# Graph convolution over 32 batches on one core: units in pairs of two batches, class rows read from 32 lanes, a ring of seven PSUM banks

## What is computed

```python
h = relu(layernorm(x, axis=-1))                 # x: 32 x 256 x 1024
# per batch: fv = h.mean(axis=1); sim = outer(fv, fv) / |fv|^2
# A = top 9 of each row of sim, without the first; symmetric; diagonal 1
y = relu((A / deg) @ (h.T @ W.T + b1))          # W = adj, 256 x 256
z = (A / deg) @ (y @ W.T + b2)
out = x + z.T
```

## Time and profile before

| | |
|---|---|
| median of 3 runs | 511.9 us (511.42 to 513.54) |
| the profiled execution | 514.48 us, of which the span is 512.7 |
| granted TensorE clock | 0.976 on the mean, 1.00 from 108 us on |
| PE busy | 449.6 us (88%) |
| VectorE busy | 428.0 us (83%) |
| ScalarE busy | 267.1 us (52%) |
| GpSimd busy | 206.4 us (40%) |
| chain that ended last | VectorE 44%, PE 23%, issue 11%, ScalarE 10%, GpSimd 8% |

### The profile page before, as it was taken

How to read it: one execution, slowest core, us unless ns; L and a number is a source line. 1 busy time by engine, 2 the same in 40 slices (tenths; PEclk the granted TensorE clock), 3 DMA queues, 4 the chain that set the end, 5 groups by cost and what they waited for, 6 DMA issues and landing times.

```text
span 512.7 us, 7375 instructions
## 1 busy us (share of the span) xinstructions
PE 449.6 (88%) x2188; PEld 200.9 (39%) x2188; DVE 428.0 (83%) x784; ACT 267.1 (52%) x561; POOL 206.4 (40%) x873
## 2 busy tenths in 40 slices
PE   0655599896998899999999899999999899999996
PEld 0112244333443344444444344444444444444442
DVE  5999879998899997999799988999799857853354
ACT  2975575347772377456863387356754453014300
POOL 1526463603537135623736335603744341414100
PEclk9986789999999999999999999999999999999999
DMA  8980000258003770087104760188006400250025
GB/s 296 383 352 1 1 1 2 82 193 291 10 1 130 256 271 1 1 319 269 71 0 166 257 236 1 58 272 320 11 0 225 168 19 1 82 216 31 1 115 214
DMA packets 19400, 68.20 MB, mean 133 GB/s; under 512 B 1824, under 2 KB 2464, under 8 KB 19360
## 3 DMA queue, kind: packets, MB, share of 16 engines
q1 hardware_dynamic: 19360, 67.73, 36.2%
HBM read 34.17 MB, written 33.55 MB: 132 GB/s over the span
## 4 chain that ended last, share of the span: by engine, by line
DVE 44%; PE 23%; issue 11%; ACT 10%; POOL 8%; POOLq 3%; DMA 1%; SPq 0%; DVEq 0%; ACTq 0%
PE ps L375 18%; DVE bn L905 10%; DVE hl L927 7%; DVE xs L946 7%; DVE hl L933 6%; POOL gat L709 4%; ACT hf L521 4%; ACT hl L530 3%; PE ps L387 3%; POOLq L706 2%; DVE idx L969 2%; DVE fv L961 2%; ACT hl L542 2%; DVE kind L978 1%; DVE fv L973 1%
## 5 line engine op out<-in xcount | busy, mean ns | idle before, releaser
L375 PE MATMUL ps<-hl,wh 128*128 128x512 f16 x1024 | 308.0, 383 | 29.6 <-DVE wl L1100 11.3
L375 PE MATMUL ps<-hl,wl 128*128 128x512 f16 x512 | 195.6, 382 | 0.0
L375 PEld LDWEIGHTS ps<-hl,wh 128*128 128x128 f16 x1024 | 97.7, 99 | 155.0 <-DVE xs L946 17.7
L521 ACT ACTIVATE hf<-xs,nbias,rstd 128x1024 f32<-128x1024 f32 x64 | 79.0, 1234 | 74.2 <-POOL nbias L695 68.9
L542 ACT ACTIVATE hl<-ps 128x512 f16<-128x512 f32 x128 | 74.9, 593 | 54.6 <-PE ps L387 54.6
L933 DVE SCALAR_TENSOR_TENSOR hl<-ps,hl 128x1024 f16<-128x1024 f32 x64 | 77.6, 1213 | 29.7 <-ACT hl L542 29.4
L927 DVE TENSOR_TENSOR hl<-hf,hl 128x1024 f16<-128x1024 f32 x64 | 77.5, 1214 | 20.7 <-ACT hl L530 20.4
L905 DVE BATCH_NORM_STATS2 bn<-xs 128x6 f32<-128x512 f32 x128 | 81.9, 678 | 5.7 <-DMA xs<-x_dram 5.7
L946 DVE SCALAR_TENSOR_TENSOR xs<-ps,sc,xs 128x1024 f32<-128x1024 f32 x62 | 77.6, 1262 | 5.9 <-PE ps L387 5.7
L375 PEld LDWEIGHTS ps<-hl,wl 128*128 128x128 f16 x512 | 50.4, 99 | 61.5 <-issue 1.9
L685 POOL TENSOR_TENSOR nw<-r 128x2 f32<-128x2 f32 x32 | 11.6, 363 | 146.6 <-DVE r L920 146.6
(11 more groups left out here) (128 smaller groups left out, 418.5 us busy)
## 6 DMA issues: line engine op xcount, KB each, us to landing
xs<-x_dram SPq DMA_DIRECT2D x62, 512.0 KB, 6.9
out_dram<-xs SPq DMA_DIRECT2D x31, 1024.0 KB, 5.0
xs<-x_dram SPq DMA_DIRECT2D x4, 256.0 KB, 3.9
out_dram<-xs SPq DMA_DIRECT2D x4, 256.0 KB, 2.1
wt<-adj_t_dram SPq DMA_DIRECT2D x1, 256.0 KB, 9.9
b1r<-b_row_dram SPq DMA_DIRECT2D x1, 128.0 KB, 10.0
b2r<-b_row_dram SPq DMA_DIRECT2D x1, 128.0 KB, 10.7
cs<-consts_dram SPq DMA_DIRECT2D x1, 86.5 KB, 9.9
```

The lines of the kernel that those rows point to most:

```text
L375: pe.matmul(ps[i % 3][:, m], w[:, k, o], hl[:, slot, part, k, cols], start=(k == 0 and w is wh and part == 0), stop=False)
L521: act.activation(hf[:, c % NHF], xs[:, n % NX, k], ACT.Relu, bias=nbias[:, n % RB, k:k + 1], scale=rstd[:, n % RB, k:k + 1], accum_out=s_a ...
```

## The change

- The order of units within a layer goes by pairs of the same half of two batches: (batch 0, half 0), (1, 0), (0, 1), (1, 1), (2, 0), (3, 0), (2, 1), (3, 1). In layer 2 of the last group the last four are (2, 0), (2, 1), (3, 0), (3, 1). `turn` gives a unit's place in that order, and the waits count turns. A batch's store and the reuse of its slot wait for both of its units (`both`).
- `rows` takes a pair: for each bank m one product for each of the two batches, which reads only that batch's 32 lanes of `lw` and `onehot`. It stands behind both mains. In the last group's layer 2 the last four units have it one by one.
- The masked copies `l1w`, `l2w` and the masks are gone: 64 instructions of VectorE less.
- One PSUM tensor of seven banks is a ring. Bank m of unit i of the whole program (`place`) is bank (2i + m) mod 7, and each half of `main` waits for the unit that last had its own bank: four units back for m = 0, three for m = 1. A unit whose banks are 6 and 0 is read by `y_lo` or `final` in two instructions; 18 of 128 are such.
- All small products share the eighth bank, `pm`. For groups from 2 on both halves of the means went through one bank before, too; in group 1 they had one each.

```diff
+RING = 7
+PAIRED = ((0, 0), (1, 0), (0, 1), (1, 1), (2, 0), (3, 0), (2, 1), (3, 1))
+LAST = ((0, 0), (1, 0), (0, 1), (1, 1), (2, 0), (2, 1), (3, 0), (3, 1))
...
+        def pieces(i):
+            first = KC * i % RING
+            return [(0, 1), (1, 2)] if first == RING - 1 else [(0, KC)]
...
             def main(layer, n, half):
...
-                if i >= 3:
-                    was, m, h = unit_of_place(i - 3)
-                    pe.wait_ge(lo2_ready if was == 1 else done, NH * m + h + 1)
...
                 for m in range(KC):
+                    was = (KC * i + m - RING) // KC
+                    if was >= 0:
+                        of = unit_of_place(was)
+                        pe.wait_ge(lo2_ready if of[0] == 1 else done, turn(*of))
...
+            def rows(*them):
+                layer, g = them[0][0], GROUP[them[0][1]]
+                pe.wait_ge(row_w, 2 * g + layer)
+                pe.wait_ge(onehot_ready, g + 1)
+                for m in range(KC):
+                    for layer, n, half in them:
+                        at = slice(LANE[n] * LANES, (LANE[n] + 1) * LANES)
+                        last = pe.matmul(bank(place(layer, n, half), m), lw[at, layer - 1, m * P:(m + 1) * P],
+                                         onehot[at, g % 2, half * HALF:(half + 1) * HALF], start=False, stop=True)
+                        if m == KC - 1:
+                            last.then_inc(l1_ps if layer == 1 else l2_ps, 1)
...
             for g in range(NG):
+                us = units(g, 0) + units(g, 1)
+                for i in range(0, len(us), 2):
+                    for u in us[i:i + 2]:
+                        if g > 0 or us.index(u) >= EARLY:
+                            main(*u)
+                    rows(*us[i:i + 2])
+                    if i == (2 if g == 0 else 0):
+                        times_q1(g)
+                    if g > 0 and i in (2, 4) and is_group(g + 1):
+                        means(g + 1, i // 2 - 1)
+                us = units(g, 2) + units(g, 3)
                 if g == 0:
                     means(1, 0)
+                main(*us[0])
+                if g == 0:
+                    means(1, 1)
+                main(*us[1])
                 times_q2(g)
+                main(*us[2])
+                rows(*us[:2])
+                main(*us[3])
+                rows(*us[2:4])
                 if is_group(g + 1):
+                    main(*us[4])
+                    main(*us[5])
+                    rows(*us[4:6])
                     plain_rows(g + 1)
+                    main(*us[6])
                     class_sizes(g + 1)
+                    main(*us[7])
+                    rows(*us[6:])
+                else:
+                    for u in us[4:]:
+                        main(*u)
+                        rows(u)
...
             def y_lo(n, half):
...
+                for piece in pieces(i):
+                    ms = slice(*piece)
+                    last = dve.scalar_tensor_tensor(hl[:, n % NHL, 1, ms, cols], banks(i, piece), 0.0,
+                                                    hl[:, n % NHL, 0, ms, cols], ALU.max, ALU.subtract)
...
             def rows_w(r):
...
-                dve.wait_ge(row_w, r + 1)
-                for b in range(GB):
-                    dve.tensor_scalar(out_w[:, b], lw[:, r % 2], cs[:, C_MINE + b:C_MINE + b + 1], None, ALU.mult
-                                      ).then_inc(ready, 1)
```

More of the change, by code:

```diff
@@ L168, in gnn_kernel @@
         lw = sb("lw", [P, 2, S], BF16)
[L169 to L173, removed]
+        ps = ctx.enter_context(nc.psum_tensor("ps", [P, RING, HALF], F32))
         pm = ctx.enter_context(nc.psum_tensor("pm", [P, HALF], F32))
@@ L267, in front, with order @@
             return n if n < stop else None
+        def order(g, layer):
+            return LAST if g == NG - 1 and layer == 2 else PAIRED
         def unit(g, i):
@@ L272, in unit, with turn, both @@
             layer, u = (1, i) if i < of else (2, i - of)
-            return layer, FIRST[g] + u // NH, u % NH
+            lane, half = order(g, layer)[u]
+            return layer, FIRST[g] + lane, half
         def units(g, q):
             return [unit(g, i) for i in range(q * SIZES[g], (q + 1) * SIZES[g])] if is_group(g) else []
+        def turn(layer, n, half):
+            g = GROUP[n]
+            return NH * FIRST[g] + order(g, layer).index((LANE[n], half)) + 1
+        def both(layer, n):
+            return max(turn(layer, n, half) for half in range(NH))
         def place(layer, n, half):
             g = GROUP[n]
-            return 2 * NH * FIRST[g] + (layer - 1) * NH * SIZES[g] + NH * LANE[n] + half
+            return NH * FIRST[g] + (layer - 1) * NH * SIZES[g] + turn(layer, n, half) - 1
         def unit_of_place(i):
@@ L365, in main @@
                 else:
-                    pe.wait_ge(lo2_ready, NH * n + half + 1)
+                    pe.wait_ge(lo2_ready, turn(1, n, half))
                     if half == 0:
@@ L393, in means @@
                 pe.wait_ge(lo_ready, KC * ends(g))
[L394 to L398, removed]
+                if half == 0:
+                    pe.wait_ge(v1_ready, KC * g)
+                else:
+                    pe.wait_ge(fv_copied, NH * g + 1)
                 for k in range(KC):
@@ L494, in _ @@
-                if is_group(g + 1):
+                    main(*us[6])
                     class_sizes(g + 1)
-                for u in fourth[3:]:
-                    main(*u)
-                    rows(*u)
+                    main(*us[7])
+                    rows(*us[6:])
+                else:
+                    for u in us[4:]:
+                        main(*u)
+                        rows(u)
         @block.scalar
```

99 lines of the change are left out of this document (32 added, 67 removed).

## The result

| | before | after |
|---|---|---|
| median, compared in the same minutes | 512.72 us (511.42 to 514.08, 4 runs) | 536.88 us (535.19 to 537.38, 4 runs) |
| the profiled execution | 514.48 us, span 512.7 | 536.85 us, span 535.1 |
| granted TensorE clock | 0.976 | 0.941 |
| PE busy | 449.6 us (88%) | 445.8 us (83%) |
| VectorE busy | 428.0 us (83%) | 417.1 us (78%) |

What follows compares the result with a forecast made beforehand. It took VectorE's chain to bound groups 1 to 5 and PE alone groups 6 and 7. Terms +1.5 (group 0), -0.7 (group 1), +4.2 (groups 2 to 5), -3.1 (6 and 7) gave +1.9: 513.8 us, range 506.5 to 522.

Steps and rivals of the forecast that it cites:

- Loads come late: Rival, third batch's slot: stored 2 us later, 2.4 us of room; four more in the queue give 521 us; chance 0.05.
- PE idles some 3 us before `class_sizes`, having nothing else queued there: Groups 2 to 5, PE ahead of the class counts: some 3 us of idle time, with no cost of its own.
- The pair's rows: PE's `rows` for two units: 0.65 us per pair instead of 0.86, with 0.22 for switching in and out.
- free switches: Rival on PE's `rows`: switching tiling costs nothing, 0.43 us per pair, 506.3 us in all; chance 0.15.
- lanes that don't overlap: Rival on PE's `rows`: 1.08 us per pair, 528 us; about 518 if partial; chance 0.2 for partial or absent overlap.
- Group 0: Turn to layer 2: unit 8's main between the means' halves delays `top_a` to 86.7, +2.6 us; +1.5 for the group.
- the first two losses of a group: Groups 2 to 5: `y_lo` 0 gets its input 0.7 us late, `y_lo` 2 loses 0.6, as paired units come together.
- The losses of 0.1 at `y_lo` 4 and 0.25 at `y_lo` 6: Groups 2 to 5: units 4 and 5 lose 0.1 us, units 6 and 7 another 0.25, reaching +0.8 in all.
- the term for a group, +1.05: Groups 2 to 5, each: +0.8 us of lateness and +0.25 of split reads; +4.2 over four groups.
- Group 1: Units 0 to 2 ready long before ScalarE needs them, no losses: -0.88 for masked copies, +0.2, together -0.7 us.
- The last groups: Groups 6 and 7, PE alone: cheaper pairs and the seventh bank save 1.6 and 1.5 us, together -3.1.
- Lateness swallowed: Rival, groups 2 to 5: VectorE's waits for h absorb late `y_lo` 0 and 2, 1.3 us per group, 508.6; chance 0.1.

Runs made afterwards that it cites:

- e1_loads: Changed kernel, with SyncE waiting for stores and issuing loads after every second batch, before the next group's results: 521.74 us, ratio 1.0140.
- e4_before_loads: Kernel before, with only the loads moved, to be issued after every second batch: 513.56 us, ratio 0.9996.
- e6_warm: Changed kernel with 18 products of no use ahead of `class_sizes`, loads and order unmoved: 534.92 us, ratio 1.0396.
- e9_loads_warm: Changed kernel with loads issued after every second batch and 10 products of no use ahead of `class_sizes`: 521.40 us, ratio 1.0135.
- e3_both: Changed kernel with loads issued after every second batch and `class_sizes` behind the rows of units 14 and 15: 512.59 us, ratio 0.9973.
- e5_all: e3_both with both halves of group 1's means one behind the other again, ahead of unit 8's main: 510.58 us, ratio 0.9939.
- e10_mixed: e5_all with single rows for units 0 to 3 of groups 1 to 5, pairs otherwise: 512.19 us, ratio 0.9979.

## Why the prediction was wrong, step by step

**The step that failed first: "Loads come late".** I had this rival and gave it 0.05. I checked the third batch of a group, whose store moved, and found 2.4 us of room. The load that mattered is another: that of the group before's fourth batch, which SyncE issues only behind the next batch's store, and that store moved from unit 9's final to unit 10's, past the gather. Its room in the kernel before was 1.0 us (7.02 less the 6.0 it took), and the move brought the issue 3.2 us nearer to the statistics. The term stood at nothing in the sum, and measured 9.1 us in groups 2 to 5 (waits of 2.19, 2.35, 1.97 and 2.54). The mechanism is shown by e1_loads (14.6 us of groups 2 to 5) against e4_before_loads (nothing).

**The step that failed second: "PE idles some 3 us before `class_sizes`, having nothing else queued there".** The idle time was forecast (2.7 in e1_loads) and taken as free. It is not: the clock falls behind it, at 5 us in five groups of five, at 2.7 to 2.8 in three of four. The price was 1.8 us per group in e6_warm, 1.5 in e1_loads. It is also the place where the order was simply worse than it could be, even at the full clock: groups without any lower clock take 56.9 us in e1_loads and 56.8 and 57.0 in e9_loads_warm, and the same groups 0.8 to 1.0 less in e3_both, with `class_sizes` behind the rows. e1_loads has no extra products, so it isn't these that cost.

The sum over groups 2 to 5: the waits for the load are 9.1 us; the four mains of unit 15 take 4.37, 4.65, 4.87 and 4.73 us from their first product to their rows, where 2.68 is the full clock's time, which is 7.9 more. That makes 17.0 of the table's 18.6 and leaves 0.4 per group, near the 0.1 to 0.3 by which the groups at the full clock in e1_loads and e9_loads_warm are longer than before. Both causes feed each other (a late load lengthens the idle time), so the split is good to some tenths.

**What held.** The pair's rows cost 0.63 to 0.64 us instead of 0.65, so both rivals on PE's switches fall, free switches (0.43) and lanes that don't overlap (1.08). "Changing tiling mode (not just tile) drains the TensorE", says the Trainium skill (TensorEngine Tiling, Key Properties); the trace agrees, with 0.10 us ahead of the rows and 0.11 behind. The Trainium skill's speedup of 3.07 for four products over 32 input lanes each side by side (TensorE: Matmul & The Clock Gate, Part 3), by which a pair would have cost 0.78, is not what two of them show here: four products took 0.53 with the switch behind them, the full factor of two.

Group 0: `top_a` of group 1 was forecast for 86.7 and began there:

```profile
86.68 1.23 DVE L980 MAX8 top<-fv 128x8 f32<-128x1032 f32 x1
```

VectorE's 51 us per group held too, and so did the first two losses of a group: at the full clock `y_lo` 0 waits 0.66 and 0.78 us in e9_loads_warm (0.7 forecast), `y_lo` 2 0.54 (0.6). The losses of 0.1 at `y_lo` 4 and 0.25 at `y_lo` 6 did not come, and the masked copies were worth 1.1 instead of 0.88. So the term for a group, +1.05, was too large: groups at the full clock are 0.1 to 0.3 longer than before. Group 1 took 0.9 to 1.0 less in e1_loads, e5_all, e9_loads_warm and e10_mixed, forecast 0.7.

**The last groups.** From unit 0's main in group 6 to the end the forecast had about 106 us instead of 109.4. The changed kernel takes 106.4 (from 428.69), e1_loads 106.3: this term held to some tenths. Counted from `class_sizes` of that group, the changed kernel is only 1.9 us better than before, because unit 15's main stands between, at the lower clock.

**"Lateness swallowed".** This rival would have made the groups some 0.2 us shorter than before (+1.05 less 1.3); they were 0.1 to 0.3 longer, and in e10_mixed 1.0 us of lateness came back as 0.9 us per group. So it did not hold there, but the measured figure lies nearer to it than to mine, and how much of the lateness at `y_lo` 0 and 2 passes on was not measured by itself.

## What to carry to other kernels

When a change reorders results, follow every transfer that is issued behind one of them, not only the transfer of the batch that moved, and read its room in the trace of before, issue to first use less issue to landing at that very place: here it was 1.0 us, and the issue moved by 3.2. Idle time of PE is not free when a run of products follows it on the chain; fill it by moving work that is due anyway in front of the wait. Products of no use cost their full time wherever PE sets the pace. And in this kernel side-by-side products were worth making throughout only where PE sets the pace; where it doesn't, ask how much later the first result of a pair comes than that of a single unit.

## What the runs showed of the hardware

Ahead of unit 15's main the granted clock fell to the 1.2 GHz level whenever PE had stood idle for 5 us (five times of five in the changed kernel), three times of four behind 2.7 to 2.8 us (e1_loads), and not when it had been busy until 1.3 us ahead (e6_warm). The length of the idle time alone doesn't decide it: behind a wait of 2.05 us for the class rows the clock fell in some groups of e3_both and e9_loads_warm and not in others, while in the kernel before it stayed at 1.00 behind 3.21 us:

```profile
127.95 0.60 PE L375 MATMUL ps<-hl,wh 128*128 128x512 f16 x2 [3.21 <-DVE hl L933]
```

Each of unit 15's mains in the changed kernel that met a fall lost 1.7 to 2.2 us. Two products over 32 input lanes each, on different lanes and different banks, ran fully side by side: four in the time of two, with 0.21 us for both switches. The 512 KB transfer read above landed 5.9 to 6.3 us after its issue in the kernel before and the changed one, where the median of all such transfers was 6.9 and 7.5, and once 8.3 us after it (e6_warm), which made the statistics behind it wait 4.6 instead of 2.4 us: a transfer with no room behind it turns this scatter into time.
